# Two attention and expert layers on one core: slot positions counted through a block matrix on TensorE, and four weight pieces split in the attention loop

## The reference

```
x = x + tanh(g_xattn[0]) * cross_attention(layernorm(x), ctx)
x = x + tanh(g_ffn[0])   * block_ffn(layernorm(x))      # 8 blocks of 32 rows of every sequence, each with weights of its own
x = x + tanh(g_xattn[1]) * cross_attention(layernorm(x), ctx)
x = x + tanh(g_ffn[1])   * moe(layernorm(x))            # 7 experts, 2 per token, and a shared one
```

```
h = layernorm(x) ; logits = h @ Wr ; top_vals, top_idx = top_k(logits, 2) ; gates = softmax(top_vals)
idx = top_idx.T.reshape(-1)
pos = sum(cumsum(onehot(idx), 0) * onehot(idx), -1) - 1      # how many earlier entries chose the same expert
keep = pos < 732
xe[idx, pos] = h                                              # scatter into slots
out = gates-weighted rows of expert(xe)  +  (silu(h @ W1s) * (h @ W3s)) @ W2s
```

## Time and profile before

| | |
|---|---|
| median of 3 runs | 925.39 us |
| the profiled execution | 927.21 us |
| its span, first to last instruction | 925.1 us |
| busy share: PE, DVE, ACT, POOL | 95%, 58%, 46%, 30% |
| mean granted TensorE clock | 0.982 |

### The profile page before, as it was taken

The page is one execution under the profiler, slowest core; times in us unless marked ns, Lnnn a source line. Parts: engine busy times, 40 slices in busy tenths (PEclk is TensorE's granted clock), DMA queues, the critical chain, the costliest instruction groups (busy, mean ns, idle before and its releaser), DMA issues.

```text
span 925.1 us, 17722 instructions
## 1 busy us (share of the span) xinstructions
PE 875.1 (95%) x5854; PEld 798.2 (86%) x5854; DVE 537.8 (58%) x1143; ACT 429.7 (46%) x938; POOL 276.5 (30%) x319
## 2 busy tenths in 40 slices
PE   8899899999969999997899999999999999999996
PEld 6677678999957778785888899999999999999985
DVE  5467665555568786658344464655647363636556
ACT  3445555777746555543134362534536261625340
POOL 6233332777765334124554002010010202020100
PEclk9899999999979999999899999999999999999998
DMA  8143124477620000011311342322322231423152
GB/s 302 24 142 120 61 100 153 151 225 226 192 72 6 7 5 5 6 48 34 107 61 41 103 126 72 108 72 91 89 67 74 85 113 50 132 65 108 42 182 91
DMA packets 74838, 86.94 MB, mean 94 GB/s; under 512 B 31188, under 2 KB 46962, under 8 KB 74668
## 3 DMA queue, kind: packets, MB, share of 16 engines
q1 hardware_dynamic: 70956, 79.86, 28.3%
q0 software_dynamic: 3552, 6.55, 2.1%
q10 hardware_dynamic: 288, 0.01, 0.0%
HBM read 64.08 MB, written 23.63 MB: 95 GB/s over the span
## 4 chain that ended last, share of the span: by engine, by line
PE 83%; DVE 5%; SPq 4%; ACT 2%; issue 2%; DMA 2%; POOL 1%; ACTq 0%; DVEq 0%; POOLq 0%
PE score L267 13%; PE score L269 13%; PE score L268 13%; PE bank_p L267 7%; PE bank_p L268 7%; PE bank_p L269 7%; PE bank L581 5%; PE score L561 4%; PE bank_p L572 3%; SPq L328 3%; PE bank L601 3%; PE bank L593 2%; PE bank L522 2%; PE bank L860 1%; DVE residual L1693 1%
## 5 line engine op out<-in xcount | busy, mean ns | idle before, releaser
L1101 ACT ACTIVATE silu<-score 128x366 f32<-128x366 f32 (+1 forms) x144 | 72.6, 504 | 286.2 <-PE score L269 286.2
L1448 DVE TENSOR_TENSOR prod<-silu,score 128x366 f32<-128x366 f32 (+1 forms) x144 | 82.0, 569 | 116.2 <-ACT silu L1101 112.5
L267 PE MATMUL score<-xe_hi,w_hi 128*128 128x366 f32 x448 | 149.1, 333 | 0.0
L269 PE MATMUL score<-xe_hi,w_lo 128*128 128x366 f32 x448 | 148.1, 331 | 0.0
L268 PE MATMUL score<-xe_lo,w_hi 128*128 128x366 f32 x448 | 148.1, 331 | 0.0
L267 PE MATMUL bank_p<-w_hi,hid_hi 128*122 128x256 f32 (+1 forms) x464 | 133.7, 288 | 9.8 <-DVE residual L1530 6.3
L1926 POOL DMA_INDIRECT slots_out<-yh,home_of x42 | 40.8, 972 | 336.6 <-DVE yh L1574 336.6
L268 PE MATMUL bank_p<-w_lo,hid_hi 128*122 128x256 f32 (+1 forms) x464 | 132.0, 285 | 0.0
L269 PE MATMUL bank_p<-w_hi,hid_lo 128*122 128x256 f32 (+1 forms) x464 | 131.8, 284 | 0.0
L267 PEld LDWEIGHTS bank_p<-w_hi,hid_hi 128*122 128x122 f32 (+1 forms) x464 | 87.7, 189 | 11.3 <-DVE residual L1530 6.5
L1765 POOL TENSOR_TENSOR w_lo<-raw,w_hi 128x512 fp32r<-128x512 f32 x62 | 82.3, 1359 | 26.6 <-ACT w_hi L927 24.9
(11 more groups left out here) (195 smaller groups left out, 1756.4 us busy)
## 6 DMA issues: line engine op xcount, KB each, us to landing
raw<-w_second_d SPq DMA_DIRECT2D x108, 256.0 KB, 2.6
raw<-w_first_d SPq DMA_DIRECT2D x72, 256.0 KB, 3.5
slot_rows<-yh SPq DMA_DIRECT2D x8, 771.0 KB, 3.4
yh<-slot_rows SPq DMA_DIRECT2D x8, 674.6 KB
v_blk<-values SPq DMA_DIRECT2D x256, 5.0 KB, 2.0
slots_out<-yh SPq DMA_DIRECT2D x8, 512.0 KB, 4.6
wa<-attn_w_d SPq DMA_DIRECT2D x8, 256.0 KB, 4.6
yh<-slots_out SPq DMA_DIRECT2D x4, 512.0 KB, 7.8
```

What stands on the lines that cost most here:

```text
L267: nc.tensor.matmul(o, a_hi, b_hi, start=start, stop=False)
L269: return nc.tensor.matmul(o, a_lo, b_hi, start=False, stop=stop)
L1101: nc.scalar.activation(silu[0:rows_n, buf, 0:width], src, ACT.Silu).then_inc(silu_done, 1)
L1448: nc.vector.tensor_tensor(prod[0:rows_n, buf, 0:width], silu[0:rows_n, buf, 0:width], up, ALU.mult).then_inc(gu_free, 1)
```

## The change

- Routing: `routing_counts` and the `cum` buffers are gone. `pick` is laid out choice, expert, tile. PE sums each (expert, tile) column over the 128 rows by two matmuls (`pick` by `ones`, one for each choice) behind gate and up f = 6; ACT copies the sums out of PSUM ahead of silu f = 7; behind f = 7 PE multiplies them with `earlier`, a matrix that marks the earlier tiles of the same expert, and adds `before` by `pick`: three matmuls where two were. DVE runs `shared_hidden(0, 4)` inside the choices and `shared_hidden(0, 5)` behind them, and works out the first slot of each expert (`routing_first`) ahead of f = 6.
- `earlier` is made on POOL behind the first attention, by a memset and three selections of up to 224 columns.
- Down pieces of chunk 0: loaded ahead of the second attention's value DMAs on SP, split in steps 3 to 6 of the second attention, on ACT at the place where the first attention does it, on POOL ahead of `rstd2_of`. The splits behind f = 3 to 6 are gone.
- Some small tiles are packed in other places (left out below).

```
@@ -161,8 +163,9 @@
...
         cand = sb("cand", [P, T, E1])
-        pick = sb("pick", [P, 2, T, E1])
-        cum = [sb(f"cum{i}", [P, 2 * T, E1]) for i in range(2)]
+        pick = sb("pick", [P, 2, E1, T])
+        part = sb("part", [P, 2, E1, T])
+        tile_sums = sb("tile_sums", [P, 2, P])
         top = sb("top", [P, 2, T])
...
@@ -234,6 +237,7 @@
...
         choice, route, e_done, pos_psum = sem("choice"), sem("route"), sem("e_done"), sem("pos_psum")
+        sums_psum, sums_kept, earlier_done = sem("sums_psum"), sem("sums_kept"), sem("earlier_done")
         puts_ready, slots_ready = sem("puts_ready"), sem("slots_ready")
...
@@ -446,8 +450,6 @@
...
                 sp.dma_start(raw[:, f, :], w_second[0, f]).then_inc(raw_in[f], 16)
-            attention_loads(1)
-
 
...
@@ -473,6 +475,7 @@
...
             pieces2(0)
+            attention_loads(1)
             pieces13(1)
...
@@ -894,13 +897,21 @@
...
 
-            for f in range(4, FT):
+            TE = T * E1
+            pick_v = pick[:].rearrange("p c e t -> p (c e t)")
+            earlier_v = earlier[:].rearrange("p c e t -> p (c e t)")
+            for f in range(4, FT - 1):
                 shared_gate_up(0, f)
             pe.wait_ge(route, 1)
-            pick_v = pick[:].rearrange("p c t e -> p (c t e)")
-            nc.tensor.matmul(bank[0][:, 0:2 * T * E1], before[:], pick_v, start=True, stop=False)
-            nc.tensor.matmul(bank[0][:, 0:2 * T * E1], ones[:], cum[1][:].rearrange("p g e -> p (g e)"),
-                             start=False, stop=True).then_inc(pos_psum, 1)
+            for c in range(2):
+                last = nc.tensor.matmul(bank[1][0:TE, c * P:(c + 1) * P], pick_v[:, c * TE:(c + 1) * TE], ones[:], start=True, stop=True)
+            last.then_inc(sums_psum, 1)
+            shared_gate_up(0, FT - 1)
+            pe.wait_ge(sums_kept, 1)
+            pe.wait_ge(earlier_done, 4)
+            nc.tensor.matmul(bank[0][:, 0:2 * TE], before[:], pick_v, start=True, stop=False)
+            nc.tensor.matmul(bank[0][:, TE:2 * TE], tile_sums[0:TE, 1, :], earlier_v[0:TE, 0:TE], start=False, stop=False)
+            nc.tensor.matmul(bank[0][:, 0:2 * TE], tile_sums[0:TE, 0, :], earlier_v[0:TE, :], start=False, stop=True).then_inc(pos_psum, 1)
             shared_down_weights(0)
...
@@ -1027,6 +1038,8 @@
...
                     nc.scalar.activation(w_hi[:, p, :], raw[:, p, :], ACT.Copy).then_inc(hi13, 1)
+                if layer == 1 and n is None:
+                    nc.scalar.activation(w_hi[:, bass.ds(b + (FT - 3), 1), :], raw[:, bass.ds(b - 3, 1), :], ACT.Copy).then_inc(hi2, 1)
                 probs_t(g, 1)
...
@@ -1063,6 +1076,9 @@
...
                 attention_step(layer, 2, 2)
+                if layer == 1:
+                    for j in range(4):
+                        act.wait_ge(raw_in[j], 16 * piece2_slot_load(0, j))
                 with act.Fori(3, B - 1) as b:
...
@@ -1206,9 +1222,11 @@
...
             for f in range(3, FT):
+                if f == FT - 1:
+                    act.wait_ge(sums_psum, 1)
+                    nc.scalar.activation(tile_sums[0:T * E1, :, :].rearrange("p c n -> p (c n)"), bank[1][0:T * E1, 0:2 * P],
+                                         ACT.Copy).then_inc(sums_kept, 1)
                 shared_silu(0, f)
-                if f < 7:
-                    split2(f - 3, piece2_slot_load(0, f - 3), FT + f - 3)
 
...
@@ -1592,48 +1610,40 @@
...
                     step(nc.vector.tensor_reduce(best[:], eq[:], AX_X, ALU.max))
-                    step(nc.vector.tensor_tensor(pick[:, c], w_bc, best[:].unsqueeze(2).to_broadcast(wide), ALU.is_equal))
-                    if c == 0:
-                        step(nc.vector.scalar_tensor_tensor(out=cand[:], in0=pick[:, 0], scalar=-3.0e38, in1=lv, op0=ALU.mult, op1=ALU.add))
+                    by_token = pick[:, c].rearrange("p e t -> p t e")
+                    picked = nc.vector.tensor_tensor(by_token, w_bc, best[:].unsqueeze(2).to_broadcast(wide), ALU.is_equal)
+                    if c == 1:
+                        picked.then_inc(route, 1)
+                    else:
+                        step(picked)
+                        step(nc.vector.scalar_tensor_tensor(out=cand[:], in0=by_token, scalar=-3.0e38, in1=lv, op0=ALU.mult, op1=ALU.add))
+                        shared_hidden(0, 4)
                 nc.vector.tensor_tensor(e_dif[:], top[:, 1, :], top[:, 0, :], ALU.subtract).then_inc(e_done, 1)
-                return steps
-
-            def routing_counts(steps):
-
-                def step(ins):
-                    steps[0] += 1
-                    ins.then_inc(choice, 1)
-                    dve.wait_ge(choice, steps[0])
-
-                flat = pick[:].rearrange("p c t e -> p (c t) e")
-                step(nc.vector.memset(cum[0][:, 0, :], 0.0))
-                step(nc.vector.tensor_copy(cum[0][:, 1:, :], flat[:, 0:2 * T - 1, :]))
-                d, at = 1, 0
-                while d < 2 * T:
-                    if d == 4:
-                        shared_hidden(0, 5)
-                    a, o = cum[at], cum[1 - at]
-                    step(nc.vector.tensor_copy(o[:, 0:d, :], a[:, 0:d, :]))
-                    ins = nc.vector.tensor_tensor(o[:, d:, :], a[:, d:, :], a[:, 0:2 * T - d, :], ALU.add)
-                    d, at = 2 * d, 1 - at
-                    if d >= 2 * T:
-                        ins.then_inc(route, 1)
-                    else:
-                        step(ins)
-                assert at == 1
+
+            def slot_step(steps, ins):
+                steps[0] += 1
+                ins.then_inc(added, 1)
+                dve.wait_ge(added, steps[0])
+
+            def of_choice(dst, src):
+                return nc.vector.tensor_reduce(dst[:].rearrange("p (c t) -> p c t", c=2), src[:].rearrange("p c e t -> p c t e"), AX_X, ALU.add)
+
+            def routing_first(steps):
+
+                dve.wait_ge(route, 1)
+                for c in range(2):
+                    last = nc.vector.tensor_tensor(part[:, c], pick[:, c], base_e[:].unsqueeze(2).to_broadcast([P, E1, T]), ALU.mult)
+                slot_step(steps, last)
+                slot_step(steps, of_choice(first, part))
 
...
                 def step(ins):
-                    steps[0] += 1
-                    ins.then_inc(added, 1)
-                    dve.wait_ge(added, steps[0])
-
-                flat = pick[:].rearrange("p c t e -> p (c t) e")
-                step(nc.vector.tensor_tensor(cum[0][:], flat, base_e[:].unsqueeze(1).to_broadcast([P, 2 * T, E1]), ALU.mult))
-                step(nc.vector.tensor_reduce(first[:], cum[0][:], AX_X, ALU.add))
+                    slot_step(steps, ins)
+
                 dve.wait_ge(pos_psum, 1)
-                step(nc.vector.tensor_tensor(cum[0][:], bank[0][:, 0:2 * T * E1].rearrange("p (g e) -> p g e", e=E1), flat, ALU.mult))
-                step(nc.vector.tensor_reduce(pos[:], cum[0][:], AX_X, ALU.add))
+                step(nc.vector.tensor_tensor(part[:].rearrange("p c e t -> p (c e t)"), bank[0][:, 0:2 * T * E1],
+                                             pick[:].rearrange("p c e t -> p (c e t)"), ALU.mult))
+                step(of_choice(pos, part))
                 step(nc.vector.tensor_scalar(keep[:], pos[:], float(CAP), None, ALU.is_lt))
...
@@ -1667,12 +1677,12 @@
...
             attention(1)
-            steps = routing_choices()
-            shared_hidden(0, 4)
-            routing_counts(steps)
+            routing_choices()
+            shared_hidden(0, 5)
+            steps = [0]
+            routing_first(steps)
             for f in range(6, FT):
                 shared_hidden(0, f)
-            steps = [0]
             routing_slots(steps)
...
@@ -1760,6 +1770,10 @@
...
                                         ALU.subtract).then_inc(lo_ready, 1)
+
+            def low_of(p, w):
+                return nc.gpsimd.tensor_tensor(w_lo[:, w, :].rearrange("p a n -> p (a n)"), raw[:, p, :].rearrange("p a n -> p (a n)"),
+                                               w_hi[:, w, :].rearrange("p a n -> p (a n)").bitcast(F32), ALU.subtract)
 
...
@@ -1784,6 +1798,10 @@
...
                     low13(PIECES0 + M0 + n, M0 + n, M0 + n)
+                if layer == 1 and (n is None or 3 <= n < B - 1):
+                    pool.wait_ge(hi2, b + (3 * E0 - 2))
+                    settle(pool)
+                    low_of(bass.ds(b - 3, 1), bass.ds(b + (FT - 3), 1)).then_inc(lo2, 1)
                 if layer == 0 and two:
...
@@ -1830,8 +1848,6 @@
...
                         shared_low(f)
-                        if f < 7:
-                            low2(3 * E0 + f - 3, f - 3, FT + f - 3)
                 else:
...
@@ -1885,6 +1901,14 @@
...
             attention(0)
+            nc.gpsimd.memset(earlier[:], 1.0).then_inc(earlier_done, 1)
+            pool.wait_ge(earlier_done, 1)
```

(22 more changed lines are left out.)

## The result

The changed kernel takes 930.57 us (median of 7 runs, 928.01 to 932.11), the kernel before 925.41 us (7 runs, 923.41 to 926.8). The ratio is 1.0049, with a 95% interval of 1.0037 to 1.0061: slower by 5.2 us, where the prediction was 922.2 us and 926.5 at most. The profiled execution took 931.14 us, with a span of 929.3.

What follows compares the result with a forecast made beforehand. PE, busy 95% of the span, was taken to bound the kernel. Routing and chunk 0 -9.8, attention split +6.6, the rest 0: -3.2 us from 925.4 gives 922.2 us (own range 920 to 924.5, overall 919.5 to 926.5).

Steps and rivals of the forecast that it cites:

- Part 1: Routing and chunk 0: PE's waits and slow clock go, some matmuls are added; -9.8 us (-10.4 to -8.8).
- The products of f = 4 and f = 5: Chunk 0, DVE: done at 426.4 and 430.1 us, in time for PE's f = 6 (427.1) and f = 7 (430.4).
- the 0.3 taken off for semaphores: Chunk 0: 0.3 us off the -10.1 gain for semaphore steps that rows do not show one by one.
- Part 2: Second attention, steps 3 to 6: POOL's new w_lo ahead of rstd2_of delays DVE and PE; +6.6 us (5.4 to 8.9).
- 0.3 for the port: Second attention: w_lo and DVE's L1280 block each other; 0.3 us a step, between 0 and 0.44.
- The lead that the prediction left open: Second attention: L1280's 0.03 us lead over w_lo decides whether a step costs 1.4 or about 1.9 us.
- The rest: earlier on POOL (1.3 to 2 us, hidden in idle time) and four more DMA issues on SP: 0 us.
- Slower: Rival: lengthened attention steps lower the clock, 2.8 us a fall; 925.0 for one, 927.8 two, 930.6 three; chance 0.06.
- the signs named ahead: If right: L1286 waits for rstd, steps 1.2 us or more longer, chunk 0 gaps under 0.5 us, down-pass clock 1.00.
- the port waits: Rival, second attention: POOL stands behind both L1280 in each step; +8.9 with -9.8, 924.5 us; chance 0.18.
- the hidden split: Rival, second attention: rstd2 still comes in time, so the split costs nothing; 915.6 us; chance 0.06.
- a routing that gives less: Rival, chunk 0: shared_down still starts at slow clock, or DVE binds f = 6 and f = 7; 925.0 us; chance 0.10.

Runs made afterwards that it cites:

- e7: The changed kernel with only ACT's split copy of steps 3 to 6 moved forward, behind the first exponential; POOL's order unchanged: 915.62 us, ratio 0.9895.
- e3: The changed kernel with POOL's w_lo of steps 3 to 6 put behind rstd2_of, ACT's part unchanged: 921.07 us, ratio 0.9958.
- e4: The changed kernel with the split of steps 3 to 6 moved, on ACT behind the first exponential, on POOL ahead of the first rstd_of: 915.91 us, ratio 0.99.
- e9: The kernel before with four more DVE operations (results thrown away) ahead of L1286 in steps 3 to 5 of the second attention: 934.75 us, ratio 1.0112.
- e6: e4 with the first attention's ACT copy and POOL w_lo moved to the same two places: 908.41 us, ratio 0.9829 against the kernel before.
- e5: The changed kernel with ten idle matmuls on PE ahead of the transposes in each of steps 3 to 6: 923.04 us, ratio 0.9967.

## Why the prediction was wrong

**Part 1, the routing and chunk 0: right.** Forecast -9.8 (-10.4 to -8.8), measured 32.77 - 22.35 = 10.4 us. The products of f = 4 and f = 5 come in time, as laid out: by DVE's timeline the second is done at 442.74 + 0.68 = 443.42, and f = 7, which needs it, begins at 443.50, with 0.08 us to spare. The sums take 0.44 us in the chain (forecast 0.6), ACT's copy of them 0.38 (0.62), hidden behind f = 7, and the three count matmuls 0.98 (1.3). The down pass starts without a wait, at 1.00, and its 96 matmuls take 11.4 us, where the forecast had 11.3. The terms that were too large by 0.1 to 0.3 us each, and the 0.3 taken off for semaphores, are about the 0.6 between -9.8 and -10.4.

**Part 2, the delay: right in its sum, less so in its terms.** Forecast 1.43 us for two steps, 0.15 less for two, and 0.3 for the port: +6.6. By the starts of L1304 behind L1298 (2.84, 2.83, 2.53 and 2.45 us, 0.90, 0.90, 0.90 and 0.98 before) it is 1.94, 1.93, 1.63 and 1.47: 7.0; by the stages, 6.7. The lead that the prediction left open was DVE's in steps 3 and 4, by 0.11 us, and there both engines paid: L1298 went from 0.87 to 1.89, `w_lo` from 1.27 (e7) to 1.50. In steps 5 and 6 it was POOL's, by 0.09 us, and DVE alone paid, 1.86 and 1.85. L1733, which is 0.20 in e7, took 0.38 in all four. The prediction put 5.4 us down to the order and 1.2 to the meeting of the two. e3, where only the meeting is left, still has 4.2 of the 6.7: the two overlap, and their sizes were not shown apart by the rows it went by.

**The rest, costed at nothing: right.** `earlier` takes a memset and two rows of selections, and POOL goes from it over one small cast into `w_lo` without a gap; the four more DMA issues on SP end 10 us ahead of the value DMAs of the second attention. From after's timelines of POOL and SP, answering:

```profile
164.45 0.28 POOL L1904 MEMSET earlier<- 128x224 f32 x1
164.81 1.01 POOL L1907 TENSOR_SCALAR_AFFINE_SELECT earlier<-earlier 128x224 f32<-128x224 f32 x2
165.89 0.32 POOL L1910 TENSOR_SCALAR_AFFINE_SELECT earlier<-earlier 128x112 f32<-128x112 f32 x1
...
166.40 3.79 POOL L1779 TENSOR_TENSOR w_lo<-raw,w_hi 128x512 fp32r<-128x512 f32 x3
```

```profile
258.02 1.85 SPq L461 DMA_DIRECT2D raw<-w_second_d  x4
269.92 2.52 SPq L332 DMA_DIRECT2D v_blk<-values  x4
```

Behind chunk 0 the rest is 470.62 us, within the 468.86 to 470.65 of the other kernels, whose code is the same there.

**The step that failed: the clock in the lengthened steps.** It stood among the rivals, as "Slower", with PE idle about 2.1 us in each of four steps, 2.8 us for each fall, and 930.6 us from three falls on; I argued against it from the earlier trace rows, where the first attention's steps keep 1.00. The measured time is 930.57, and in the profiled execution the four waits are 2.06 to 2.44 us, each has a fall behind it, and a fall costs 1.6 to 3.3 us, 2.1 on average. So the term that the sum put at nothing was +8.3 us: -10.4 + 6.7 + 8.3 = +4.6, where the spans differ by 4.2. That the rival's 930.6 is met to 0.1 us is luck in part, as three falls of its 2.8 us are as much as four of 2.1. The argument took the earlier trace rows for proof, and it failed twice. PE's wait in the earlier trace rows is 1.82 us, and my own sum put the new wait at 2.1, beyond every wait in that attention behind which the clock had held. And that the clock held there was itself the luck of one execution: in the same step of the same code it fell in four of the eleven traces. A warning was at hand: the waits of the earlier trace rows and the 2.82 us of the earlier trace rows end in the 0.53 of the earlier trace rows.

Of the signs named ahead, all of the right ones appeared, among them L1304 waiting for `rstd` and steps more than 1.2 us longer. The list asked for 1.00 in the down pass, and never for the clock in the attention, where the rival lived.

The other rivals: the port waits (924.5) exist, but the delay beyond the 5.4 us of the order is 1.3 to 1.6 us for all four steps, and not 3.5; the hidden split (915.6) is what e4 and e7 do at 915.9 and 915.6 us, by another place and not by slack in this one; a routing that gives less did not occur.

## What to carry to other kernels

When a change lengthens PE's waits, price the clock as well as the delay: here 6.7 us of delay came with 8.3 us of slow clock, as four waits went from 0.5 to over 2 us. A stretch in which the clock held is no proof that it will: look at waits of the same length, in more than one execution, before a term is put at nothing. Work that an idle-looking engine takes over must be laid against what is queued behind it there and against which operations of the neighbour it meets; the same two instructions cost nothing 4.6 us earlier in the step. And idle matmuls in a wait that can't be removed are a cheap test, and here a cure, of the clock's part.

## What was not expected of the hardware

- PE's waits of 1.97, 1.97 and 1.98 us, in three steps with the same instructions, were followed by 1.00, 1.00 and a fall (e9), and four executions of that kernel spread over 5.4 us, while those of e4 spread over 1.1 us. After's seven runs go from 928.01 us at a mean clock of 0.983 to 932.11 at 0.974.
- Behind the same wait of 1.82 to 1.83 us of the first attention the clock fell in four of eleven traces, and behind one of 2.68 us for a DMA (e6) it did not.
- Falls of one kernel do not cost the same: 1.7, 1.7, 3.3 and 1.6 us in after. The one at the wait of 5.98 us at the start of the second attention left 0.66 granted from 264 to 284 us in before and after, and 0.83 in e5.
- When DVE's pair and POOL's `w_lo` meet, it costs 1.0 us of DVE (0.87 to 1.89) and 0.23 us of POOL (1.27 to 1.50), with DVE ahead by 0.11 us. Where POOL was first, in step 0 of the earlier trace rows and in steps 5 and 6 of after, its `w_lo` kept 1.28, and DVE's pair took 1.85 to 1.89. Whether POOL work that reads no SBUF would spare DVE this, was not tried.
